# From experts to attention batch by batch: the order of norm, K, Q and V at the turn between two layers

## The chip, the cores and the metric

The kernel runs on one core of a Trainium2 chip. The metric is the device time in microseconds, the median of three executions. The engines are PE (matrix multiply), DVE (vector), ACT (scalar), POOL (GpSimd) and SP (here it issues DMAs only). Each takes its instructions in the order in which they are written, and they meet through semaphores.

## The reference

Two layers over x of shape (2, 512, 256). Layer 0 is a Mamba-2 block multiplied by a mixture of 8 experts; layer 1 is attention with rope, 32 query heads and 8 key and value heads of width 64, multiplied by a sign network.

```
xn = layernorm(x)
s = ssm(xn)                       # chunked selective scan
g = silu(experts(xn))             # top 2 of 8
x = x + s * g                     # end of layer 0
xn = layernorm(x)
q, k, v = xn @ Wq.T, xn @ Wk.T, xn @ Wv.T
q, k = rope(q), rope(k)
attn = softmax(causal(q @ k.T / sqrt(64)))
s = (attn @ v) @ Wo.T
a = sign(layernorm(x) * gamma + beta)
g = silu((a @ sign(W - mean(W)).T + bias) * alpha)
x = x + s * g
```

## The kernel before

Tokens lie in 8 tiles of 128 rows (`NT`), four to each of the two batches. Matmuls that need fp32 accuracy are split in three (`split3`): a value is written as a high and a low part, ACT copies the high part out of a PSUM bank, DVE or POOL subtracts it from the value for the low part, and PE multiplies low by high, high by low and high by high.

At the turn from layer 0 to layer 1 PE sums the experts' rows for four pairs of tiles (`sum_pair`), ACT applies silu to each pair (`gated`), DVE multiplies with the scan's result and adds to x (`add_pair`), and takes the statistics of the norm (`pair_stats`, `norm_spread`). The square root is ACT's, between DVE's `rsqrt_asked` and `rsqrt_made`. DVE then writes all 8 tiles of xn1; PE turns them (`turn_norm`), ACT and DVE make xnT_hi and xnT_lo (`lower_norm`). PE then makes K, Q and V of batch 0 for the first head group, then K and V of batch 1, and only then attention begins.

Attention is `attend(now, steps)`, called for each of the 8 head groups (a key head and its four query heads). All engines walk the same list `schedule(kind)`; each takes from it the operations that are its own. A step has a number and a priority, and the list is sorted by both. "Sab" is a matmul of scores for pair a (two heads of a batch; pairs 2 and 3 are batch 1), step b of 5. E is the exponential on ACT, N the reciprocal on DVE and the normalization on POOL, T the turn of prob on PE with its p_hi copy on ACT and p_lo on DVE, A the product with V. Beside these run the preparations: Q, r, a, h, l are the matmuls, rope, addition, high part and low part of later queries; Kh and Kl the high and low part of k_exp, which SP brings by DMA; Kq, Kr, Ka make K of head groups 4 to 7; KW and VQ split weights, F and G prepare the sign network's rows. `x_roped` says that a bank of PE has been taken by rope, and PE may not write it before.

SP's queue has a fixed order too: `spread_k` copies k to the four partition groups of k_exp (four DMAs), `store_k` and `store_v` put K and V in DRAM for later groups, `move_q` moves q_hi and q_lo to the layout qT (eight DMAs each), `load_wq` brings weights. In the first group of before batch 1's q is moved after all of these.

Of the kernel before, what the change touches and what calls it, by code (L numbers as in the profile page):

```python
# [72 lines left out]
def schedule(kind):  # L73

    own = [(14, 0, "VO", 0, 0), (1, 8, "Kh", 1, 0), (2, 6, "Kl", 1, 0)]
# [19 lines left out]
    if kind == "first":  # L95
        ready += [(0, 7, "KW", 0, 0), (3, 0, "VQ", 0, 0)] + half(1, 0, 1) + half(2, 7, 0) + half(3, 13, 0)
        for b in range(BATCH):
            n = 3 + 7 * b
            for k in range(2):
                ready += [(n + k, 8.2, "Kq", b, k), (n + k + 1, 8.2, "Kr", b, k), (n + k + 4, 6.2, "Ka", b, k)]  # L100
        ready += [(1 + t, 8.95, "F", t, 0) for t in range(NT)]
# [13 lines left out]
def side_by_side():  # L115
# [19 lines left out]
    z += [(4 * NJ + 0.5, "ACT", "kv", 0), (4 * NJ + 0.6, "POOL", "kv", 0)]  # L135
    z += [(4 * NJ + 0.1 * n, "DVE", "sum", n) for n in range(NT // 2)]
# [27 lines left out]
def layered_kernel(nc, x, params, consts, select, rope, w_in, w_out, w_moe, w_moe_tail, w_qkv, w_o, w_sign, out):  # L164
# [4 lines left out]
    with ctx:  # L169
# [301 lines left out]
        def _(sp):  # L471
# [74 lines left out]
            def move_q(g, b):  # L546

                hh = g * 2 + b
                for src, done in ((q_hi, qhi_done), (q_lo, qlo_done)):
# [14 lines left out]
            def spread_k(g, b):  # L564

                hh = g * 2 + b
                if hh > 0:
                    sp.wait_ge(klo_done, hh)
# [51 lines left out]
            move_q(0, 1)  # L620
# [30 lines left out]
        def _(dve):  # L651
# [22 lines left out]
            def rsqrt_asked(src, eps):  # L674
                TS(root_arg, src, eps, None, ALU.add).then_inc(var_ready, 1)

            def rsqrt_made(dst, ready=None):

                roots[0] += 1
                dve.wait_ge(root_ready, roots[0])  # L680
                then(vec.reciprocal(dst, root))
                then(TT(sv[:, 3, :], root_arg, dst, ALU.mult))
                then(TT(sv[:, 3, :], sv[:, 3, :], dst, ALU.mult))
                then(TS(sv[:, 3, :], sv[:, 3, :], -0.5, 1.5, ALU.mult, ALU.add))
                if ready:
                    TT(dst, dst, sv[:, 3, :], ALU.mult).then_inc(ready, 1)
                else:
                    then(TT(dst, dst, sv[:, 3, :], ALU.mult))
# [5 lines left out]
            root_arg, root = sv[:, 0, :], sv[:, 2, :]  # L694
# [326 lines left out]
            def attend(now, steps):  # L1021
                for late, op, i, k in steps:
# [22 lines left out]
                    elif op == "O":  # L1045
                        b, m = i // 2, i % 2
                        dve.wait_ge(ohi_done, q + 1)
                        TT(o_lo[:, b, m, :], bank[4 + m][:, :], o_hi[:, b, m, :].bitcast(F32), ALU.subtract).then_inc(olo_done, 1)  # L1048
# [17 lines left out]
            dve.wait_ge(turns_ready, 1)  # L1066
            dve.wait_ge(vpad_ready, 4)
            lower_norm(0)
            lower_norm(1)
            for k in range(2):  # L1070
# [5 lines left out]
            lower_norm(2)  # L1076
# [5 lines left out]
            ins.then_inc(q_first, 1)  # L1082
            lower_norm(3)
            TT(q_lo[:, :, :], q_mix[:, :, 0, :], q_hi[:, :, :].bitcast(F32), ALU.subtract).then_inc(qlo_done, 2)
            for k in range(2):
                rope_k(0, 1, k, bank[4 + k])
            rsqrt_made(rrms, second_ready)
            for b in range(BATCH):
                lower_v(0, b)
# [20 lines left out]
        def _(act):  # L1110
            actv = nc.scalar.activation

            def root(n):
                act.wait_ge(var_ready, n + 1)
                actv(sv[:, 2, :], sv[:, 0, :], ACT.Sqrt).then_inc(root_ready, 1)
# [125 lines left out]
            for n in range(NT // 2):  # L1241
                act.wait_ge(mixed, n + 1)
                actv(gate_y(n), gate_y(n), ACT.Silu).then_inc(gated, 1)
                if n == 1:
                    act.wait_ge(turns_full, 1)
                if n > 0:
                    ins = actv(turns[:, n - 1, :], bank[n - 1][:, :], ACT.Copy)
            ins.then_inc(turns_ready, 1)
            actv(sv[:, 8, :], ones[:, 0:NT], ACT.Sqrt)
            act.wait_ge(turns_full, 2)  # L1250
            actv(wsT[:, :, :], bank[4][:, :].rearrange("p (k o) -> p k o", k=KC), ACT.Copy).then_inc(turns_ready, 1)
# [17 lines left out]

            def upper_k(now, i):  # L1270
# [6 lines left out]
            def attend(now, steps):  # L1277
                for late, op, i, k in steps:
# [3 lines left out]
                    if op == "E":  # L1282
# [4 lines left out]
                        if k == 0 and isinstance(g, int) and q < 2:  # L1287
                            act.wait_ge(k_out[q], 16)
# [50 lines left out]
            root(2)  # L1339
            split_wq(0)  # L1340
            for k in range(KC * BATCH):
                b, c = k // KC, k % KC
# [629 lines left out]
```

## Time and profile before

| what | us |
|---|---|
| median of 3 runs | 773.09 |
| lowest, highest | 772.72, 774.26 |
| the profiled execution | 774.21 |
| its span | 772.4 |
| PE busy | 716.3 (93%) |
| DVE busy | 487.4 (63%) |
| ACT busy | 416.8 (54%) |
| POOL busy | 397.1 (51%) |

Mean granted clock 0.982. The span is the time from the first to the last instruction. Busy shares are means over stages; the expert stage takes about the first 300 us, and the attention groups fill the time from 345 us to the end.

### The profile page before, as it was taken

How to read it: one execution, taken by the hardware profiler on the slowest of the kernel's cores; microseconds unless marked ns; L12 is line 12 of the kernel's file. 1: busy time of each engine (PE TensorE's matmuls, PEld its weight loads, DVE VectorE, ACT ScalarE, POOL GpSimd, SP SyncE). 2: the span in 40 equal slices, each digit the busy share in tenths (PEclk: the TensorE clock that was granted, in tenths of full speed). 3: DMA queues.
4: the chain of work that ended last, by engine and by line, in shares of the span. 5: the costliest groups of instructions: out<-in, count | busy, mean ns of one | idle time of the engine just before them, and what ended most of it. 6: DMA issues, size and time to landing. Idle time of an engine off the chain costs nothing.

```text
span 772.4 us, 13448 instructions
## 1 busy us (share of the span) xinstructions
PE 716.3 (93%) x4575; PEld 625.0 (81%) x4576; DVE 487.4 (63%) x1030; ACT 416.8 (54%) x1043; POOL 397.1 (51%) x449
## 2 busy tenths in 40 slices
PE   2999999999999998588789999999999999999995
PEld 2887989989989986566678888888888888888883
DVE  7582655334332437876557777777777778777764
ACT  4446244134144133447367777667766677667663
POOL 1412442422332323118577786767867778677460
PEclk9899999999999999899899999999999999999999
DMA  8075977776877744154134222332223322232001
GB/s 295 31 249 183 277 251 233 246 245 203 280 241 214 244 98 118 27 168 121 60 94 112 58 63 65 84 89 52 64 63 90 85 55 64 52 90 56 1 1 55
DMA packets 103828, 98.06 MB, mean 127 GB/s; under 512 B 50576, under 2 KB 74064, under 8 KB 103632
## 3 DMA queue, kind: packets, MB, share of 16 engines
q1 hardware_dynamic: 101648, 91.43, 40.8%
q0 software_dynamic: 2112, 5.77, 2.3%
q8 instruction: 37, 0.61, 0.3%
q14 instruction: 31, 0.25, 0.1%
HBM read 69.24 MB, written 11.14 MB: 104 GB/s over the span
## 4 chain that ended last, share of the span: by engine, by line
PE 63%; DVE 12%; POOL 10%; ACT 8%; issue 4%; SPq 2%; DMA 1%; DVEq 0%; ACTq 0%; POOLq 0%
PE bank L1656 14%; PE bank L1516 8%; PE bank L1690 7%; PE bank L1517 7%; PE bank L1518 7%; PE bank L1512 7%; POOL prob L1474 5%; ACT prob L1290 3%; PE bank L1796 3%; DVE nmax L1035 2%; PE bank L1797 2%; POOL q_lo L1486 2%; ACT p_hi L1297 2%; DVE o_lo L1048 1%; POOL wq_lo L1454 1%
## 5 line engine op out<-in xcount | busy, mean ns | idle before, releaser
L1474 POOL TENSOR_TENSOR prob<-prob,rinv 128x128 f32<-128x128 f32 (+3 forms) x256 | 177.6, 724 | 102.9 <-DVE rinv L1040 102.9
L1290 ACT ACTIVATE prob<-bank,nmax 128x512 f32<-128x512 f32 (+3 forms) x256 | 133.2, 528 | 45.3 <-DVE nmax L1035 43.8
L1044 DVE TENSOR_TENSOR p_lo<-bank,p_hi 128x512 fp32r<-128x512 f32 x160 | 110.0, 687 | 52.8 <-ACT p_hi L1297 51.9
L1297 ACT ACTIVATE p_hi<-bank 128x512 fp32r<-128x512 f32 x160 | 96.3, 602 | 79.3 <-PE bank L1512 79.3
L1656 PEld LDWEIGHTS bank<-xgT,wm 128*128 128x128 f32 x920 | 108.7, 192 | 4.5 <-issue 2.9
L1656 PE MATMUL bank<-xgT,wm 128*128 128x128 f32 x920 | 111.3, 275 | 0.5 <-ACT xgT L1199 0.5
L1512 PE MATMUL bank<-cst,prob 128*128 128x128 f32 x640 | 97.9, 276 | 3.0 <-POOL prob L1474 1.2
L1035 DVE TENSOR_REDUCE nmax<-bank 128x1 f32<-128x512 f32 (+2 forms) x192 | 91.0, 502 | 12.7 <-PE bank L1799 12.1
L1516 PE MATMUL bank<-p_hi,v_lo 128*128 128x128 f32 (+3 forms) x256 | 93.0, 363 | 0.3 <-DVE p_lo L1044 0.3
L1796 PE MATMUL bank<-kT,qT 128*128 128x512 f32 (+3 forms) x256 | 82.2, 326 | 11.6 <-ACT prob L1290 6.0
L1445 POOL DMA_INDIRECT y_rows<-y_row,to_row x21 | 22.7, 1081 | 118.3 <-DVE y_row L904 92.6
L1518 PE MATMUL bank<-p_hi,v_hi 128*128 128x128 f32 (+3 forms) x256 | 82.4, 322 | 0.0
L1517 PE MATMUL bank<-p_lo,v_hi 128*128 128x128 f32 (+3 forms) x256 | 82.3, 322 | 0.0
L1512 PEld LDWEIGHTS bank<-cst,prob 128*128 128x128 f32 x640 | 73.7, 142 | 6.0 <-POOL prob L1474 3.3
L1797 PE MATMUL bank<-kT,qT 128*128 128x512 f32 (+3 forms) x256 | 74.7, 323 | 0.0
L1796 PEld LDWEIGHTS bank<-kT,qT 128*128 128x128 f32 x256 | 48.4, 189 | 21.8 <-issue 7.6
L1224 ACT ACTIVATE sil<-bank 128x512 f32<-128x512 f32 x23 | 13.7, 596 | 76.0 <-PE bank L1656 54.5
L1690 PE MATMUL bank<-wm,hE 128*128 128x256 f32 x230 | 53.5, 379 | 1.2 <-DVE y_low L909 1.2
L1290 ACT ACTIVATION_READ_ACCUMULATOR prob<-bank,nmax 128x1 f32 x256 | 52.4, 205 | 0.0
L944 DVE TENSOR_TENSOR hE<-sil,bank 128x512 f32<-128x512 f32 x23 | 15.8, 687 | 57.6 <-PE bank L1656 40.6
L1797 PEld LDWEIGHTS bank<-kT,qT 128*128 128x128 f32 x256 | 48.6, 190 | 3.9
L1518 PEld LDWEIGHTS bank<-p_hi,v_hi 128*128 128x128 f32 x256 | 48.4, 189 | 2.8
(307 smaller groups left out, 1544.6 us busy)
## 6 DMA issues: line engine op xcount, KB each, us to landing
wm<-in_w_moe SPq DMA_DIRECT2D x23, 1280.0 KB
wm<-in_w_moe SPq DMA_DIRECT2D x23, 640.0 KB
qT<-q_hi SPq DMA_DIRECT2D x124, 64.0 KB, 2.0
qT<-q_lo SPq DMA_DIRECT2D x124, 64.0 KB, 2.0
k_exp<-k_rows SPq DMA_DIRECT2D x56, 64.0 KB, 2.0
wtl<-in_w_moe_tail SPq DMA_DIRECT2D x46, 64.0 KB
y_rows<-gate SPq DMA_DIRECT2D x1, 2048.0 KB, 14.1
wq_raw<-in_w_qkv SPq DMA_DIRECT2D x32, 64.0 KB, 2.5
```

What stands on the lines that cost most here:

```text
L1044: TT(p_lo[:, b_, :], bank[2 + b_ % 2][:, :], p_hi[:, b_, :].bitcast(F32), ALU.subtract).then_inc(plo_done, 1)
L1290: ins = actv(prob[:, i % 2, h, POFF[j]:POFF[j] + (j + 1) * P], bk[:, at:at + (j + 1) * P], ACT.Exp, bias=nmax[:, i % 2, h, j:j + 1], accum ...
L1297: actv(p_hi[:, b_, :], bank[2 + b_ % 2][:, :], ACT.Copy).then_inc(phi_done, 1)
L1474: ins = GT(seg, seg, rinv[:, i % 2, k, j:j + 1].to_broadcast([P, (j + 1) * P]), ALU.mult)
L1512: return nc.tensor.transpose(dst, src, ident)
L1516: mm(dst, w_l, m_h, start=start, stop=False)
L1517: mm(dst, w_h, m_l, start=False, stop=False)
L1518: return mm(dst, w_h, m_h, start=False, stop=stop)
L1656: ins = mm(dst, w(c), xgT[:, u, c, :], start=c == 0, stop=c == KC - 1)
L1690: ins = mm(bank[3][:, 0:C], hE[:, u, i * P:(i + 1) * P], wm[:, s, i, PJ:WM] if i < FULL else ptl[:, s, :], start=i == 0, stop=i == HC - 1)
L1796: mm(dst, qs, kT[:, b, 0, 0:n], start=(h, j, at) == SCORES[k][0], stop=False)
L1797: mm(dst, qs, kT[:, b, 1, 0:n], start=False, stop=False)
```

## The change

The norm of layer 1 is split in halves, one for each batch. `half_norm` and `half_rows` do for four tiles what `norm_spread` and the loop over xn1 did for eight; batch 0's statistics, root and rows stand before the addition of pair 3, batch 1's after the rope of batch 0's K and Q. PE turns batch 0, makes its K, Q and V, turns batch 1 and begins attention. K and V of batch 1 are steps of the first group (K1, R1, A1, Vp, V1). The lows of wk0 go from POOL to DVE and those of wv0 behind xn's first half. Turns of the rope tables and their ACT copies stand behind the sums and gates of all pairs. The addition of batch 1's first q goes from POOL to DVE. SP moves q_hi of batch 1 before it spreads K of batch 1, and q_lo after. Kh and Kl of batch 1 go from steps 1 and 2 to 7 and 8, KW from 0 to 5, Kq from 3 and 10 to 8 and 14. K of batch 1 gets an area of its own (`k1_mix`, over o_lo).

```
-    own = [(14, 0, "VO", 0, 0), (1, 8, "Kh", 1, 0), (2, 6, "Kl", 1, 0)]
+    own = [(14, 0, "VO", 0, 0)]
+    own += [(7, 8, "Kh", 1, 0), (8, 6, "Kl", 1, 0)] if kind == "first" else [(1, 8, "Kh", 1, 0), (2, 6, "Kl", 1, 0)]
...
+        ready += [(1, 8.9, "R2", 0, 0), (1, 8.6, "V1", 0, 0), (6, 8.6, "V1", 1, 0)]
+        for k in range(2):
+            ready += [(1 + k, 8.1, "K1", 1, k), (2 + k, 8.1, "R1", 1, k), (3 + k, 6.1, "A1", 1, k)]
+        ready += [(2 + t - TB, 8.3, "Vp", t, 0) for t in range(TB, NT)]
...
-    z += [(4 * NJ + 0.1 * n, "DVE", "sum", n) for n in range(NT // 2)]
+    z += [(4 * NJ + 4 * (n // BATCH) + 0.1 * n, "DVE", "sum", n) for n in range(NT // 2)]
...
             store_v(0)
+            load_wq(1)
+            move_q(0, 1, (0,))
+            spread_k(0, 1)
             store_k(0, 1)
-            spread_k(0, 1)
+            move_q(0, 1, (1,))
             store_v(1)
-            load_wq(1)
...
-            move_q(0, 1)
...
+            def half_norm(b):
+                ts = slice(b * TB, (b + 1) * TB)
+                dve.wait_ge(stat_ready, NT + (b + 1) * TB)
+                for t in range(b * TB, (b + 1) * TB):
+                    vec.bn_aggr(mv[:, t, :], stats[:, t, :]).then_inc(aggr_ready, 1)
+                dve.wait_ge(aggr_ready, NT + (b + 1) * TB)
+                rsqrt_asked(mv[:, ts, 1], 1e-5, ts)
+
+            def half_rows(b):
+                rsqrt_made(rstd, None, slice(b * TB, (b + 1) * TB))
+                for t in range(b * TB, (b + 1) * TB):
+                    TS(xn1[:, t, :], x_tok[:, t, :], mv[:, t, 0:1], rstd[:, t:t + 1], ALU.subtract, ALU.mult).then_inc(xn_ready, 1)
...
+                        if q == 0:
+                            dve.wait_ge(k_out[1], 16)
+                            dve.wait_ge(k_in, 2 * K_MOVES)
...
+                    elif op == "a" and now == 0 and i == 1 and k == 0:
+                        dve.wait_ge(x_roped[1], 2)
+                        TT(q_mix[:, :, 0, :], q_mix[:, :, 0, :], q_mix[:, :, 1, :], ALU.add).then_inc(qadd_done, 2)
...
-            for k in range(KC * BATCH):
-                turn_norm(k, xn_ready, bank[k])
+            turn_half(0)
             pe.wait_ge(lo_done, KC * BATCH + 2)
             pe.wait_ge(w_lo_done, 4)
...
             for t in range(TB):
                 make_v(t)
-            pe.wait_ge(lo_done, 2 * KC * BATCH)
-            pe.wait_ge(kx_roped, 2)
-            for k in range(2):
-                make_k(0, 1, k, bank[4 + k])
-            for t in range(TB, NT):
-                make_v(t)
+            turn_half(1)
...
+                        if q < 2 and k == 0:
+                            pe.wait_ge(v_copied, NT)
```

The order of PE around the begin of attention. Before, the last V matmuls of batch 0 are followed by K of batch 1:

```order
L1516 MATMUL bank<-wv_hi,xnT_lo 128x512
L1517 MATMUL bank<-wv_lo,xnT_hi 128x512
L1518 MATMUL bank<-wv_hi,xnT_hi 128x512
L1516 MATMUL bank<-xnT_hi,wk_lo 128x512 [waits kx_roped,lo_done]
L1517 MATMUL bank<-xnT_lo,wk_hi 128x512
```

After, they are followed by the turns of batch 1 and the first scores (kT, qT):

```order
L1563 MATMUL bank<-wv_hi,xnT_lo 128x512
L1564 MATMUL bank<-wv_lo,xnT_hi 128x512
L1565 MATMUL bank<-wv_hi,xnT_hi 128x512
L1559 MATMUL bank<-cst,xn_132 128x128 [waits xn_ready]
L1559 MATMUL bank<-cst,xn_132 128x128
L1559 MATMUL bank<-cst,xn_132 128x128 [waits xn_ready]
L1559 MATMUL bank<-cst,xn_132 128x128
L1559 MATMUL bank<-cst,xn_132 128x128 [waits xn_ready]
L1559 MATMUL bank<-cst,xn_132 128x128
L1559 MATMUL bank<-cst,xn_132 128x128 [waits xn_ready]
L1559 MATMUL bank<-cst,xn_132 128x128
L1851 MATMUL bank<-kT,qT 128x512 [waits klo_done,q_first,exp_done,v_copied,mask_ready]
```

The 36 matmuls of K and V of batch 1 moved behind the first scores.

The order of ACT in the first group. Before, the high part of batch 1's K (kT<-k_exp) comes after the second exponential:

```order
L1290 ACTIVATE prob,rsum<-bank,nmax 128x384 [waits max_ready]
L1290 ACTIVATE prob,rsum<-bank,nmax 128x128
L1275 ACTIVATE kT<-k_exp 128x512 [waits k_in]
L1327 ACTIVATE xn_132<-xn_132,sv 128x256 [waits second_ready]
L1290 ACTIVATE prob,rsum<-bank,nmax 128x256 [waits max_ready]
```

After, it comes behind the exponential of the eighth score step, ahead of a p_hi copy:

```order
L1342 ACTIVATE p_hi<-bank 128x512 [waits av_done,pt_full]
L1335 ACTIVATE prob,rsum<-bank,nmax 128x256 [waits max_ready]
L1335 ACTIVATE prob,rsum<-bank,nmax 128x256
L1320 ACTIVATE kT<-k_exp 128x512 [waits k_in]
L1376 ACTIVATE xn_132<-xn_132,sv 128x256 [waits second_ready]
L1342 ACTIVATE p_hi<-bank 128x512 [waits av_done,pt_full]
L1335 ACTIVATE prob,rsum<-bank,nmax 128x512 [waits max_ready]
```

Its place moved six steps down.

The order of SP's queue. Before, k_exp of batch 1 (source prob) comes early and q_hi of batch 1 last:

```order
L601 DMA v_rows<-v_all 128x4x512 [waits v_copied]
L562 DMA k_rows<-prob 256x1x512 [waits kadd_done]
L571 DMA k_exp<-prob 32x512 [waits klo_done]
L571 DMA k_exp<-prob 32x512 x3
L601 DMA v_rows<-v_all 128x4x512 [waits v_copied]
L585 DMA wq_raw<-in_w_qkv 128x4x32 [waits wqlo_done]
L585 DMA wq_raw<-in_w_qkv 128x4x32 x3
```

After, it is behind the weights and the eight moves of q_hi:

```order
L611 DMA v_rows<-v_all 128x4x512 [waits v_copied]
L595 DMA wq_raw<-in_w_qkv 128x4x32 [waits wqlo_done]
L595 DMA wq_raw<-in_w_qkv 128x4x32 x3
L564 DMA qT<-q_hi 32x512 [waits qhi_done]
L564 DMA qT<-q_hi 32x512 x7
L581 DMA k_exp<-k_mix 32x512 [waits klo_done,kadd_done]
L581 DMA k_exp<-k_mix 32x512 x3
L570 DMA k_rows<-k_mix 256x1x512 [waits kadd_done]
L564 DMA qT<-q_lo 32x512 [waits qlo_done]
L564 DMA qT<-q_lo 32x512 x7
```

The two moves of q now enclose the transfer of batch 1's K.

## Rows read from the trace of the kernel before

**Rows 1.** Busy time by stretch, all engines; then clock, DMA share, GB/s.
```profile
390.00:402.00 12.00, 9.09 (x64) 7.53 (x63) 6.73 (x13) 6.04 (x20) 11.70 (x13) 1.00 0.26 68
550.00:600.00 50.00, 49.37 (x317) 43.07 (x316) 37.88 (x75) 35.40 (x99) 38.17 (x45) 1.00 0.28 70
```

**Rows 2.** Waits of PE from 296 to 346 us: total, times, longest.
```profile
PE bank L1512 <- DVE xn L988: 7.9, 1, 7.9
PE bank L1516 <- DVE xnT_lo L997: 2.4, 1, 2.4
PE bank L1722 <- DVE y_low L909: 1.1, 1, 1.1
```

**Rows 3.** Waits of PE from 340 to 402 us.
```profile
PE bank L1796 <- DMA qT<-q_lo: 4.7, 1, 4.7
PE bank L1512 <- DVE q_mix L1002: 2.9, 2, 1.8
```

**Rows 4.** PE by stretches of 2 us: busy, clock, DMA share, GB/s.
```profile
314.00:316.00 2.00, 0.00 (x0) 0.51 0.00 0
...
374.00:376.00 2.00, 2.00 (x9) 0.50 0.11 42
...
378.00:380.00 2.00, 2.00 (x13) 0.77 0.00 0
```

**Rows 5.** Instructions in order of time, 305 to 346 us: start, duration, idle before.
```profile
305.08 0.60 ACT L1247 ACTIVATE turns<-bank 128x512 f32<-128x512 f32 x1 [0.73 <-PE bank L1512]
...
315.47 2.67 DVE L988 TENSOR_SCALAR xn<-x_tok,mv,sv 128x256 f32<-128x256 f32 x8
...
320.35 0.74 PE L1516 MATMUL bank<-xnT_hi,wk_lo 128*128 128x512 f32 x1
...
321.39 1.28 ACT L1346 ACT_TABLE_LOAD   x1
...
327.62 2.51 SPq L571 DMA_DIRECT2D k_exp<-prob  x4
327.80 1.23 DVE L1075 TENSOR_TENSOR q_mix<-q_mix 128x1024 f32<-128x1024 f32 x1
...
330.65 2.54 ACT L1353 ACTIVATE qT<-q_mix 32x512 fp32r<-32x512 f32 x4
...
333.92 1.27 POOL L1458 TENSOR_TENSOR kT<-k_exp,kT 128x512 fp32r<-128x512 f32 x1 [6.32 <-ACT kT L1275]
334.20 2.07 DVE L1084 TENSOR_TENSOR q_lo<-q_mix,q_hi 128x1024 fp32r<-128x1024 f32 x1
...
345.38 0.47 PE L1796 MATMUL bank<-kT,qT 128*128 128x512 f32 x1 [0.83 <-ACTq L1363]
```

**Rows 6.** The same, first head group, 345 to 398 us.
```profile
345.95 0.47 PE L1516 MATMUL bank<-xnT_hi,wq_lo 128*128 128x512 f32 x1
...
347.42 0.34 PE L1796 MATMUL bank<-kT,qT 128*128 128x384 f32 x1
...
349.07 0.58 ACT L1290 ACTIVATE prob<-bank,nmax 128x384 f32<-128x384 f32 x1
...
353.75 0.68 DVE L1001 TENSOR_TENSOR v_all<-bank,turns 128x512 f32<-128x512 f32 x1
...
355.01 2.75 POOL L1474 TENSOR_TENSOR prob<-prob,rinv 128x128 f32<-128x128 f32 x4
...
357.82 0.66 PE L1512 MATMUL bank<-cst,prob 128*128 128x128 f32 x4 [1.20 <-POOL prob L1474]
...
360.25 1.06 ACT L1268 ACTIVATE q_hi<-q_mix 128x1024 fp32r<-128x1024 f32 x1 [3.45 <-POOL q_mix L1483]
...
361.34 4.95 SPq L556 DMA_DIRECT2D qT<-q_hi  x8
...
397.71 0.66 PE L1512 MATMUL bank<-cst,xn 128*128 128x128 f32 x4 [1.80 <-DVE q_mix L1002]
```

**Rows 7.** The chain that ended last, at 371 us: start, duration, what.
```profile
371.02 2.04 DMA qT<-q_lo
```

More of the change, by code:

```diff
@@ L374, in layered_kernel @@
         o_hi = attn("o_hi", [P, 2, 2, HALF], F32R)
+        k1_mix = Map(attn.at)("k1_mix", [P, 2, 2, HALF])
         o_lo = attn("o_lo", [P, 2, 2, HALF], F32R)
         def k_mix(r, b):
+            if r == 0 and b:
+                return k1_mix[:, :, :, :]
             if r == 0:
@@ L544, in _, with move_q @@
             sp.wait_ge(s_part, NT)
-            def move_q(g, b):
+            def move_q(g, b, parts=(0, 1)):
                 hh = g * 2 + b
-                for src, done in ((q_hi, qhi_done), (q_lo, qlo_done)):
+                for src, done in [((q_hi, qhi_done), (q_lo, qlo_done))[i] for i in parts]:
                     at = 0 if src is q_hi else 2
@@ L672, in _, with rsqrt_asked, rsqrt_made @@
             roots = [0]
-            def rsqrt_asked(src, eps):
-                TS(root_arg, src, eps, None, ALU.add).then_inc(var_ready, 1)
-            def rsqrt_made(dst, ready=None):
+            def rsqrt_asked(src, eps, ts=slice(0, NT)):
+                TS(sv[:, 0, ts], src, eps, None, ALU.add).then_inc(var_ready, 1)
+            def rsqrt_made(dst, ready=None, ts=slice(0, NT)):
+                arg, more, to = sv[:, 0, ts], sv[:, 3, ts], dst[:, ts]
                 roots[0] += 1
                 dve.wait_ge(root_ready, roots[0])
[L681 to L684, printed above, removed]
+                then(vec.reciprocal(to, sv[:, 2, ts]))
+                then(STT(out=more, in0=to, scalar=-0.5, in1=arg, op0=ALU.mult, op1=ALU.mult))
+                then(TT(more, more, to, ALU.mult))
+                last = STT(out=to, in0=more, scalar=1.5, in1=to, op0=ALU.add, op1=ALU.mult)
                 if ready:
-                    TT(dst, dst, sv[:, 3, :], ALU.mult).then_inc(ready, 1)
+                    last.then_inc(ready, 1)
                 else:
-                    then(TT(dst, dst, sv[:, 3, :], ALU.mult))
+                    then(last)
             def rsqrt(dst, src, eps):
@@ L1082, in _ @@
             ins.then_inc(q_first, 1)
+            lower_norm(2)
             lower_norm(3)
             TT(q_lo[:, :, :], q_mix[:, :, 0, :], q_hi[:, :, :].bitcast(F32), ALU.subtract).then_inc(qlo_done, 2)
-            for k in range(2):
[L1086 to L1089, printed above, removed]
             attend(0, schedule("first"))
@@ L1243, in _, with turned @@
                 actv(gate_y(n), gate_y(n), ACT.Silu).then_inc(gated, 1)
[L1244 to L1248, printed above, removed]
-            actv(sv[:, 8, :], ones[:, 0:NT], ACT.Sqrt)
-            act.wait_ge(turns_full, 2)
-            actv(wsT[:, :, :], bank[4][:, :].rearrange("p (k o) -> p k o", k=KC), ACT.Copy).then_inc(turns_ready, 1)
+            actv(sv[:, 8, :], ones[:, 0:NT], ACT.Sqrt)
+            def turned():
+                act.wait_ge(turns_full, 2)
+                actv(wsT[:, :, :], bank[4][:, :].rearrange("p (k o) -> p k o", k=KC), ACT.Copy)
+                for i in range(3):
+                    ins = actv(turns[:, i, :], bank[i][:, :], ACT.Copy)
+                ins.then_inc(turns_ready, 1)
             def split_wq(g):
@@ L1349, in _ @@
             upper_q(0, 0)
+            root(3, slice(TB, NT))
+            upper_k(0, 0)
             for i in range(2):
@@ L1354, in _ @@
             ins.then_inc(q_first, 1)
-            upper_k(0, 0)
-            for t in range(2, NT):
-                copy_v(t)
-            act.wait_ge(vpad_ready, 4)
-            for b in range(BATCH):
-                ts = slice(b * TB, (b + 1) * TB)
-                act.wait_ge(v_copied, (b + 1) * TB)
-                actv(v_hi[:, ts, HD:2 * HD], v_all[:, ts, 0:HD], ACT.Copy).then_inc(vhi_done, 1)
+            copy_v(2)
+            copy_v(3)
+            upper_norm(1)
+            root(4)
+            actv(sv[:, 8, :], ones[:, 0:NT], ACT.Exp)
             act.sem_inc(exp_done, 2)
@@ L1498, in _ @@
             lower_k(0, 0)
-            for k in range(2):
-                add_k(0, 1, k)
             attend(0, schedule("first"))
```

134 lines of the change are left out of this document (85 added, 49 removed).

## The prediction

> **What bounds the kernel now.** I read the busy time by stretch first. From 550 to 600 us the matmul engine is busy 49.4 of 50 us at full clock; from 390 to 402 it is busy only 9.1 of 12 while POOL works 11.7 [rows 1]. So the attention groups after the first are bound by the matmul engine, and a delay or a gain at the end of the first group goes straight to the end. All that the change touches lies between 298 and 402 us, and there the engine has gaps. The waits of the matmul engine name them: 7.9 us for the normalized rows xn, 2.4 us for xnT_lo of the second batch, 1.1 us for y_low [rows 2]; in the first group 4.7 us for the transfer of q_lo, 2.9 us for q_mix [rows 3], 1.2 us for prob [rows 6]. That is 20 us. A second loss goes with them: the clock granted in the gap is 0.51 at 314 us, 0.50 at 374 us after the 4.7 us wait, and back at full between 378 and 380 us [rows 4]; 0.5 is the 1.2 GHz level of the two, 1.0 the 2.4 GHz level.
>
> **How I count.** The chain is followed in order of each engine's instructions, each with its duration in the trace, to four points that both kernels share. I write "Sab" for the scores of pair a, step b. Before: first K matmul at 320.35, S00 at 345.38 [rows 5], S20 (first scores of batch 1) at 371.02 + 2.04 = 373.1 [rows 3, 7], end of G10, the second turn of the sign rows, 398.1 (its turns begin at 397.71 [rows 6]).
>
> **Part 1, up to K.** DVE writes y_low before the sums of pairs 2 and 3, so PE's 1.1 us wait goes [rows 2]: PE is through with the sums at about 308.0 instead of 309.1. wk_lo on DVE has no row; between half of q_mix's 1.23 us, 0.6, and the whole of q_lo's 2.07 [rows 5] I take 0.7, by the nearer. It puts off the first add by 0.6 us. Norm of batch 0 alone: two adds per pair, four statistics, then rows at 0.33 us each (2.67 us for 8) instead of eight rows [rows 5]. They are ready at about 311.1 (with the dearer wk_lo 312.1). But ACT now does gates 2 and 3, the 1.28 us table load, the first wq copy, wsT and the three turns copies at 0.60 us [rows 5] before PE may turn anything: 306.5 + 0.6 + 1.3 + 0.4 + 0.6 + 0.6 + 1.8 = 311.8. ACT's copies, not the norm, end this wait. Eight turns (1.8 at the lower clock), two hi copies, two lo subtractions: K starts at 315.9, **4.45 us earlier**.
>
> **Part 2, up to S00.** K, Q, V of batch 0 take 11.6 us as before, so PE is at 327.5 and turns batch 1 by 329.6. It then waits for ACT. Counted from kadd: the four k_exp issues 2.51 and landing 2.04 [rows 5, 7] give k_in at 327.7; ACT then does kT 0.6, the qT copies 2.54, two V copies 1.1, two hi copies 1.2, the root 0.2 and the Exp table load 1.28 + 0.2: 335.0 to 335.2 [rows 5]. Only then is exp_done raised. So S00 at **335.0, 10.4 us earlier**, with PE idle 5.4 us before it, and K1 and V of batch 1 (36 matmuls at 0.235, 8.5 us) still to be done. The 2.4 us wait of rows 2 goes, and this one stands in its place: net 1.9 us at this point.
>
> **Part 3, S00 to T00 (first turn of prob).** Before it was 12.4 us. Now, from S00 as zero: a score step takes PE 0.57, six matmuls 1.47 (345.38, 345.95, 347.42) [rows 5, 6]. PE's own work up to S11 is done at 15.4. But DVE has from S01 on six scores' maxima, four rope pairs at 1.28 [rows 6], q_mix at 1.23 [rows 5], lower_v 0.4 and the small ops 0.9: S04's maximum at 13.7. ACT follows: exponentials of S04 to 14.75 (a two part one 1.0), V copy, xn2, E10 to 16.7, the wk copies 1.3, q_hi 1.06 [rows 6] to 19.1, and the last V copy to 19.7. T00 now waits for all eight V copies. T00 at 19.75, that is **354.8, 3.0 us earlier** than 357.8 [rows 6], while 12 matmuls of Kq (2.8 us) that stood before it are now behind: even. PE is idle 4.3 us.
>
> **Part 4, T00 to S20.** SP issues q_hi of batch 1 first: 8 at 0.62 are 4.95 us [rows 6], then spread_k(0,1) 2.5, landing 2.04: k_in at 19.1 + 9.6 = 28.7. On ACT the Kh of batch 1 stands behind the third exponentials of pair 1, reached at 24.5. It is an in-order engine, so it waits 4.3 us, and behind it are the p_hi copy of T02 and E13. Before, that Kh found its data at once. What waits for ACT: p_lo on DVE at 31.2, then N10 and rope of Q20 to 32.6, and PE's Kq00, which now stands right behind Q21 (done at 26.2): PE idle 6.4 us. Then Kq00, S14, T03, A01 to 35.9, and Kq01 waits for the rope of Q21, behind S14's maximum and T03's p_lo: 37.85. S20 at 39.3, that is 335.0 + 39.3 = **374.3, 1.2 us later** than 373.1. The q_lo transfer, now landed at 34.4, no longer sets it.
>
> **Part 5, S20 to G10.** Before 25.0 us, 2.6 of them lost to the lower clock [rows 4]. Now PE needs 12 us up to Q31, but POOL needs N11 2.75, two adds 2.5, kT 1.27, Ka 1.27, N20 2.75, two q_lo 2.5 [a normalization is 2.75, rows 6] from 2.5 us on, plus a rope: 17.4. Kq10 stands right behind Q31 and waits for that rope: 5 us. Before, the sign turns were what waited there, 1.1 and 1.8 us in all, with eight other steps already done. Kq11 waits 2.0 us more, and G10 1.4 for the rope of Kq11. From S20 27.9 us: **2.9 us more**.
>
> **Sum.** 1.2 + 2.9 = 4.1 us later, before the clock. Gaps of 5.4 and 6.4 us are as long as those after which rows 4 show half clock for 4 to 5 us after work resumes (320.35 is still low, 378 too); matmuls that the chain waits for are then some 1.5 + 2.5 us late, if all of it counts, nothing if DVE and ACT hide it; I take 1. The profiled execution took 774.21 us (span 772.4), so it would take 779.3; the median of the runs is 773.09, so I forecast **778.5 us**. The cost of the DVE wait for k_out1 at the first o_lo, and of the new k1_mix area, is nothing: both transfers land 10 us before. Bounds of the unknown: PE waits and the lower clock fully hidden, 1.2 - 2.6 + 774 = 772; everything in full, 4.1 + 4 + 2 = 783.
>
> **A port.** q_lo on DVE took 2.07 us beside a POOL subtraction of 1.27 us that had started 0.28 us earlier, where q_mix of the same size alone took 1.23 [rows 5]. The Trainium skill, page "SBUF — State Buffer", section "Who interferes with whom", says that a DVE instruction with two SBUF inputs and a GpSimd one that reads SBUF exclude each other for the whole instruction. The trace agrees: the end of q_lo is the end of POOL plus 1.1. The change moves the q_mix addition of batch 1 from POOL to DVE, beside POOL's wq_lo and normalization. By the row alone I price it at 1.23. By the rule it could cost up to 1.3 us more on the chain of part 3, and the sum would be 779.8; I leave it out since POOL by my count is still waiting for wq then.
>
> **Rivals.**
> 1. The gaps are filled (faster). K1 and V of batch 1 are 8.5 us of work laid into a group that had 8.8 us of named gaps, and S00 is 10.4 us earlier. For it: [rows 1, 3]. It needs ACT to reach Kh after k_in, that is the in-order wait of part 4 to be absent; then S20 is bound by q_lo at 335 + 34.4 = 369.4, 3.7 us earlier, and with part 5 even the time is 769.4. With every gap filled it gains 10.4 - 8.5 + 8.8 = 10.7 us: 762.4; half of that, 767.7, is as far as I let the range go. Against it: the queue order on SP, eight issues of 0.62 us ahead of spread_k. 0.29.
> 2. Nothing (within 0.2%, 1.5 us, about what a measurement can tell from none): the 3.7 us of rival 1 and the 2.9 us of part 5 cancel: 772 to 774.5. 0.09.
> 3. The forecast, 774.6 to 781: 0.47.
> 4. The clock. PE is left idle five times for about 4 us and more (3.8, 5.4, 4.3, 6.4, 5) instead of twice, and each stretch after it runs at 0.5; then the matmuls of parts 3 and 4 are on the chain and it is 781 to 785. For it, rows 4; against it, PE has slack there. 0.15.
>
> So faster 0.29, same 0.09, slower 0.62. Range 767 to 783.
>
> **What would show it.** Right: K from about 316, S00 near 335 with an idle of some 5 us before it ended by ACT; T00 near 355 released by an ACT V copy; an idle of ACT of 3 to 5 us before a kT copy, ended by the k_exp transfer; PE waiting 4 to 7 us for DVE's q_mix before wk matmuls, twice; S20 at 373 to 378. Wrong: if the kT copy finds its data there, if S20 is at 370 or before, or if the matmuls of the wk half follow Q without a wait. If S00 is later than 338, part 2 is what failed.

## The result, and the profile after

The changed kernel takes 783.74 us against 772.90 us (medians of four executions of each), ratio 1.0151 (95% interval 1.0126 to 1.0177): 10.8 us slower. I had forecast 778.5 us, range 767 to 783. The sign was right, the size was half of it, and the median lies just outside the range. The profiled execution took 783.04 us, its span is 781.2 us against 772.4, mean granted clock 0.977 against 0.982.

The waits of PE in the changed kernel, in the order of the three stretches 296 to 330, 330 to 372 and 372 to 420 us (total, times, longest), to be laid beside [rows 2, 3]:

```profile
PE bank L1559 <- ACT turns L1288: 3.0, 1, 3.0
PE bank L1563 <- DVE xnT_lo L1008: 1.8, 1, 1.8
PE bank L1559 <- DVE xn L1002: 1.4, 2, 0.8
...
PE bank L1563 <- DVE q_mix L1013: 5.4, 2, 4.1
PE bank L1851 <- DVE qT L1123: 3.0, 1, 3.0
PE bank L1559 <- ACT v_all L1299: 2.9, 1, 2.9
...
PE bank L1563 <- DVE q_mix L1013: 7.4, 2, 6.0
PE bank L1559 <- DVE v_all L1013: 1.3, 1, 1.3
```

The 7.9 us for xn [rows 2] and the 4.7 us for q_lo [rows 3] are gone. In their place stand three waits of some 3 us (turns, qT, v_all) and four before the wk matmuls (L1563 <- q_mix, 12.8 us). PE's clock in stretches of 2 us (busy, clock, DMA share, GB/s), to be laid beside [rows 4]:

```profile
328.00:330.00 2.00, 0.00 (x0) 0.73 0.00 0
330.00:332.00 2.00, 1.09 (x3) 0.50 0.00 0
332.00:334.00 2.00, 2.00 (x6) 0.50 0.00 0
...
364.00:366.00 2.00, 2.00 (x5) 0.50 0.40 98
366.00:368.00 2.00, 2.00 (x8) 0.50 1.02 397
368.00:370.00 2.00, 2.00 (x10) 0.53 0.33 127
...
392.00:394.00 2.00, 2.00 (x6) 0.50 0.90 328
394.00:396.00 2.00, 2.00 (x9) 0.50 0.39 98
```

After the waits for qT (3.0 us) and before the wk matmuls (4.1 and 6.0 us) PE works 5 to 6 us at 1.2 GHz (granted clock 0.50 of full), with full busy time and fewer matmuls: 5 to 10 in 2 us.

One table holds the study. It takes the starts of three score steps in each profiled execution: S00, S20 (batch 1's first scores) and S00 of the next head group ("next"). The last column is what remains to the end of the span. "First y_lo" is the start of DVE's first y_lo in the expert stage, far ahead of the norm, K, Q and V that the change reorders; it shows how late an execution already was there.

| kernel | ratio to before, interval | first y_lo | S00 | S00 to S20 | S20 to next | next to end |
|---|---|---|---|---|---|---|
| before | | 91.74 | 345.38 | 27.7 | 33.1 | 366.2 |
| changed | 1.0151 (1.0126 to 1.0177) | 89.90 | 330.91 | 42.0 | 38.4 | 369.9 |
| changed, again | 1.0165 (1.0135 to 1.0195) | 89.81 | 331.96 | 41.9 | 39.7 | 369.7 |
| wk steps back | 0.9962 (0.9950 to 0.9974) | 89.73 | 330.72 | 36.6 | 33.1 | 366.4 |
| only batch 0's back | 1.0103 (1.0078 to 1.0127) | 91.35 | 333.80 | 35.9 | 39.5 | 369.8 |
| only batch 1's back | 1.0035 (1.0015 to 1.0054) | 89.77 | 330.79 | 42.1 | 32.1 | 366.0 |
| store last | 1.0140 (1.0113 to 1.0167) | 89.75 | 332.19 | 41.9 | 39.7 | 369.3 |
| additions behind | 1.0238 (1.0219 to 1.0258) | 89.86 | 331.46 | 41.7 | 40.5 | 376.2 |
| additions and store behind | 1.0132 (1.0101 to 1.0164) | 89.88 | 332.29 | 41.7 | 40.5 | 366.4 |
| v_lo later | 1.0152 (1.0130 to 1.0173) | 89.80 | 332.17 | 42.0 | 39.8 | 369.8 |
| K and V before the scores | 1.0020 (1.0007 to 1.0032) | 89.79 | 345.30 | 28.5 | 33.1 | 366.3 |
| lows moved, in before | 1.0003 (0.9988 to 1.0018) | 90.22 | 343.75 | 27.8 | 33.0 | 366.4 |
| wk back, spread first | 0.9968 (0.9952 to 0.9984) | 89.68 | 332.14 | 36.4 | 32.7 | 366.4 |
| the same, filled | 0.9976 (0.9960 to 0.9992) | 89.63 | 332.04 | 36.4 | 32.7 | 366.3 |
| wk back, early q | 0.9901 (0.9878 to 0.9924) | 93.19 | 334.25 | 32.2 | 31.6 | 366.4 |
| the same, and kT | 0.9866 (0.9845 to 0.9887) | 89.83 | 332.04 | 30.7 | 31.4 | 366.4 |

The changed kernel is 14.5 us ahead at S00, loses 14.3 us up to S20, 5.3 us up to the next group, and 3.7 us after it. But 1.8 of the 14.5 us are not the change's. The first y_lo of the kernel before, of the kernel before with the lows moved, of the changed kernel, and of the run with early q:

```profile
91.74 0.68 DVE L890 TENSOR_TENSOR y_lo<-gate,y_hi 128x512 fp32r<-128x512 f32 x1
```

```profile
90.22 0.68 DVE L890 TENSOR_TENSOR y_lo<-gate,y_hi 128x512 fp32r<-128x512 f32 x1
```

```profile
89.90 0.68 DVE L901 TENSOR_TENSOR y_lo<-gate,y_hi 128x512 fp32r<-128x512 f32 x1
```

```profile
93.19 0.68 DVE L901 TENSOR_TENSOR y_lo<-gate,y_hi 128x512 fp32r<-128x512 f32 x1
```

Kernels with the same code up to this row differ here by up to 3.6 us, so this is a difference between executions. Taken off, the changed kernel is 12.6 us ahead at S00, and 14.3 + 5.3 + 3.7 - 12.6 makes 10.6 us slower, which agrees with the 10.8 us of the medians. S00 is comparable between rows of the table only with the first y_lo subtracted.

### The profile page after: what moved, and what is told of

It reads as the page before. It is cut to its first block, busy times and chain, and to the rows that moved or that the text cites. A ratio compares the mean times of both kernels' runs of the same rounds, so it can differ in the third digit from the quotient of the medians.

```text
span 781.2 us, 13456 instructions
## 1 busy us (share of the span) xinstructions
PE 719.2 (92%) x4575; PEld 626.9 (80%) x4576; DVE 486.0 (62%) x1033; ACT 416.9 (53%) x1044; POOL 393.6 (50%) x446
## 4 chain that ended last, share of the span: by engine, by line
PE 64%; DVE 12%; POOL 9%; ACT 8%; issue 4%; DMA 1%; SPq 1%; DVEq 0%; ACTq 0%
PE bank L1703 14%; PE bank L1737 8%; PE bank L1563 8%; PE bank L1564 7%; PE bank L1565 7%; PE bank L1559 7%; POOL prob L1519 5%; ACT prob L1335 3%; PE bank L1851 3%; DVE nmax L1046 3%; PE bank L1852 2%; POOL q_lo L1531 2%; ACT p_hi L1342 2%; DVE o_lo L1062 2%; DVE q_mix L1012 1%
## 5 line engine op out<-in xcount | busy, mean ns | idle before, releaser
L1563 PE MATMUL bank<-p_hi,v_lo 128*128 128x128 f32 (+3 forms) x256 | 93.2, 364 | 0.3 <-DVE p_lo L1055 0.3
```

Source lines behind the costliest of these rows:

```text
L1563: mm(dst, w_l, m_h, start=start, stop=False)
```

## The experiments

**The wk steps.** The step table again as before for the second K projection:

```
-        ready += [(5, 7, "KW", 0, 0), ...
-            n = 8 + 6 * b
+        ready += [(0, 7, "KW", 0, 0), ...
+            n = 3 + 7 * b
```

> The changed kernel with the steps of the second K projection (matmuls, rope, additions) and of the wk split where they stood in the kernel before (3 + 7b and 0 instead of 8 + 6b and 5). Theory (places of the projection): the two waits of PE before those matmuls of batch 1 (6.0 and 1.4 us) go and the K additions are done before group 1, so 2.9 us of the stretch from S20 to G10 and the 2.6 us in group 1 come back: 778 us. Rival (resources): the same ropes, additions and 24 matmuls only press into the first steps, where K and V of batch 1 now stand; PE waits there for wk_low and for rope, and it is not faster: 784 to 788 us.

Measured 770.12 us, ratio 0.9962: 13.6 us under the changed kernel's 783.74, 8 us better than the theory said, and faster than the kernel before. These step numbers, of the second K projection and of the wk split, are what made the change slow. Its waits from 296 to 420 us:

```profile
PE bank L1851 <- POOL kT L1503: 5.8, 1, 5.8
...
PE bank L1559 <- DVE q_mix L1013: 2.9, 2, 1.8
```

No wait before the wk matmuls (L1563 <- q_mix) is in the list any more. Then each batch alone, `n = 3 + 11 * b` (wk split at 0) and `n = 8 + 2 * b`:

> The changed kernel with the second K projection of batch 0 (matmuls, rope, additions) back at step 3 and the wk split at step 0, as before, but that of batch 1 left at step 14. With both back, S20 came at 367.34 instead of 372.95 and S00 of group 1 at 400.43 instead of 411.34. Theory (two terms of like size): the batch 0 part is worth the 5.6 us up to S20, the batch 1 part the rest, 5.3 us up to group 1 and 2.6 us in it; this kernel then has S20 near 367.5, waits 5 to 6 us before the wk matmuls of batch 1 and takes 783.7 - 5.6 = 778.1 us. Rival (only the late additions count): S20's gain is eaten by the next POOL chain, and it takes 782 us or more.

> The changed kernel with only the second K projection of batch 1 back at step 10; batch 0 stays at step 8 and the wk split at 5. Theory (two terms): S20 stays at 373 or is up to 2 us later, since matmuls and ropes of both batches now stand close together behind Q of pair 2, but the wait of 6.0 us before the wk matmuls of batch 1 after Q31 goes, and POOL's additions end before group 1, so its T03 turn does not wait for prob: 783.7 - 5.3 - 2.6 + 1 = 777 us. Rival (crowding): the two projections together push S20 as far as the later wait was long; 783 us.

Measured 781.08 us and 776.41 us. In the table batch 0's return is worth 6.1 us between S00 and S20; batch 1's 6.3 us between S20 and the next group, and 3.8 us after it. Two separate terms, as the theory said, the second the larger. The first median lies between the theory (778.1) and its rival (782 or more): by the ratios (1.0103 against 1.0151) batch 0's return is worth 3.7 us, not 6.1. Of the 6.1 us 1.1 are given back in the next stretch (39.5 against 38.4), and from the first y_lo to S00 this execution took 242.5 us where the changed kernel's took 241.0 and, when repeated, 242.2: scatter, whose cause stays open. The second median is near its theory (777), but its 12 runs lie in two bunches 4 us apart, and its row in the table is of the faster.

**The loss behind the first group.** In the changed kernel the last steps of the wk work end up in group 1. POOL and ACT there (start, duration, idle before); v_all<-v_all are the two additions of K, which has its area there:

```profile
411.14 2.76 POOL L1519 TENSOR_TENSOR prob<-prob,rinv 128x128 f32<-128x128 f32 x4 [8.47 <-DVE rinv L1051]
413.86 1.30 POOL L1508 TENSOR_TENSOR v_all<-v_all 128x512 f32<-128x512 f32 x1
415.10 2.55 POOL L1531 TENSOR_TENSOR q_lo<-q_mix,q_hi 128x512 fp32r<-128x512 f32 x2
417.61 1.28 POOL L1508 TENSOR_TENSOR v_all<-v_all 128x512 f32<-128x512 f32 x1
418.85 1.29 POOL L1499 TENSOR_TENSOR wq_lo<-wq_raw,wq_hi 128x512 fp32r<-128x512 f32 x1
420.10 2.75 POOL L1519 TENSOR_TENSOR prob<-prob,rinv 128x128 f32<-128x128 f32 x4
...
423.48 0.63 ACT L1320 ACTIVATE kT<-k_exp 128x512 fp32r<-128x512 f32 x1 [5.82 <-DMA k_exp<-k_rows]
```

Two rows on SP's queue stand between the second addition (v_all) and that kT copy:

```profile
418.92 0.58 SPq L570 DMA_DIRECT2D k_rows<-v_all  x1
419.54 2.27 SPq L581 DMA_DIRECT2D k_exp<-k_rows  x4
```

So two suspects: the queue (the spread stands behind a store that waits for an addition) and POOL's order (the additions stand ahead of a normalization, that of the second head of pair 3, for which PE waits 2.6 us). First the queue:

```
-            store_k(1, 1)
             spread_k(1, 1)
             load_v(1, 1)
             load_wo(1)
+            store_k(1, 1)
```

> The changed kernel with one thing altered: on the SP queue the store of the last K quarter (second four head groups, batch 1) stands behind the K spread, the V load and the wo load of group 1, not ahead of them. Theory (queue): in group 1 ACT waited 5.8 us for k_exp only because that store waits for POOL's last K addition and the spread stands behind it; then k_exp lands some 3 us earlier, the POOL normalization and the turns of group 1 no longer slip, and the time falls by the 2.6 us which the milestones of group 1 lost between S03 and S04 (+5.1 to +7.7): 781.1 us, ratio to the changed kernel 0.9966. Rival (POOL): the four K additions now stand in POOL's order so late that its first normalization of group 1 is late whatever the queue does; then 783.7 us.

Measured 784.19 us, the rival's time: no gain. ACT's wait of 5.8 us is gone from its trace, the prob wait still has 2.6 us. My theory of the queue fell; next to end it is worth 0.4 to 0.6 us. Then POOL's additions of batch 1 moved behind a normalization in group 1, the store still last:

```
                         ins.then_inc(prob_ready, 1)
+                        if now == 1 and not late and q == PAIRS and k == 0:
+                            for j in range(2):
+                                add_k(1, 1, j)
```

> The changed kernel with its late second K projection kept, the last K store behind the loads of group 1 on SP (as in the run with the store last), and besides the two K additions of batch 1 on POOL behind the first normalization of group 1 instead of ahead of it. The run with the store last took ACT's 5.8 us wait for k_exp away and gained nothing. Theory (POOL's order): the 2.6 us wait of PE for prob in group 1 comes from q_lo, two additions and wq_lo ahead of that normalization; without the additions it ends 2.5 us earlier, the wait is 0 to 0.3 us and the time 783.7 - 2.6 = 781.1 us (the rest of what is lost lies before group 1). Rival: the wait only moves to the next normalization, or to kT low behind it, and the time stays at 783.7 us.

Measured 791.68 us. The prob wait went, but neither theory came: this condition puts the additions one normalization later than I meant (at 428.66), the store waits for them, and the eight moves of q_hi that stand behind it on SP start at 434.29. PE then:

```profile
445.81 0.79 PE L1854 MATMUL bank<-kT,qT 128*128 128x512 f32 x1 [7.81 <-DMA qT<-q_lo]
```

It shows the queue's price when something is needed behind it. Last, the additions directly behind the normalization that PE waits for, and the store behind the whole of group 1's queue:

> The changed kernel with its late second K projection kept, its two K additions of batch 1 on POOL directly behind the normalization that PE waits for in group 1 (second head of pair 3), and the K store that needs them behind the whole DMA order of group 1 on SP. Theory (POOL's order is the cause of that wait, SP's queue only passes a late addition on): the prob wait of 2.6 us goes, no wait for q_lo comes (8 issues start near 423 as in the changed kernel), and the time is 2.6 us under the changed kernel on the same chip, 781 us. Rival (the wait moves to the following normalization or kT low, which the additions now delay by 2.5 us): no gain, 783.7 us.

> The changed kernel itself, on the chip of the run beside it. Expected: 783.7 us, ratio to the kernel before 1.0151. If it is 782 or below or 786 or above, the differences of 1 to 3 us that I took between runs of different chips need their intervals read with more care.

Measured 782.07 and 785.23 us. Waits of PE from 404 to 470 us, first of the changed kernel again, then of this one:

```profile
PE bank L1559 <- POOL prob L1519: 2.6, 1, 2.6
PE bank L1851 <- ACT prob L1335: 1.7, 4, 0.7
PE bank L1559 <- DVE v_all L1013: 1.3, 1, 1.3
```

```profile
PE bank L1563 <- DVE v_all L1014: 1.3, 1, 1.3
PE bank L1855 <- ACT prob L1336: 1.0, 3, 0.5
```

The repeated changed kernel lies within the 782 to 786 us that I had set. Next to end is 366.4 us, as before, where it is 369.3 with the store alone moved and 369.7 in the changed kernel again. So the loss behind the first group is POOL's order, but for the 0.4 us of the store. The medians fall by 3.2 us, near the theory's 2.6, but their intervals (1.0135 to 1.0195 and 1.0101 to 1.0164) overlap: it is the distance in the traces that shows it. S20 to next is 0.8 us longer in this run; that was not followed up.

**The wait at kT.** v_lo of batch 1 on DVE at step 11 instead of 6:

> The changed kernel with one DVE instruction moved: v_lo of batch 1 at step 11 instead of step 6. Beside POOL's q_lo it took 3.30 us instead of about 0.4. Theory (my prediction's part 4): the maximum of S12 comes 2.9 us earlier, but ACT then reaches its kT copy earlier and waits there for k_exp, 3 to 4 us instead of 0.83; the time stays within 0.5 us of the changed kernel: 783.7 us. Rival (the port is the chain): the queue was not the limit, S20 comes 2.5 to 3 us earlier and the time is 781 us.

Measured 785.19 us, the changed kernel's time within the intervals. The two kernels' rows for v_lo and kT, changed kernel first:

```profile
354.53 3.30 DVE L1024 TENSOR_TENSOR v_lo<-v_all,v_hi 128x256 fp32r<-128x256 f32 x1 [0.60 <-ACT v_hi L1313]
...
360.32 0.63 ACT L1320 ACTIVATE kT<-k_exp 128x512 fp32r<-128x512 f32 x1 [0.83 <-DMA k_exp<-k_mix]
```

```profile
362.24 0.63 ACT L1320 ACTIVATE kT<-k_exp 128x512 fp32r<-128x512 f32 x1 [4.09 <-DMA k_exp<-k_mix]
...
379.10 0.77 DVE L1024 TENSOR_TENSOR v_lo<-v_all,v_hi 128x256 fp32r<-128x256 f32 x1
```

The wait of 4.3 us that I predicted is there (4.09) as soon as v_lo is out of the way. It needs no edit, though: in the second profiled execution of the changed kernel, with v_lo in its old place, v_lo took 0.83 us and the wait is there too:

```profile
356.14 0.83 DVE L1024 TENSOR_TENSOR v_lo<-v_all,v_hi 128x256 fp32r<-128x256 f32 x1 [0.59 <-ACT v_hi L1313]
```

```profile
361.93 0.63 ACT L1320 ACTIVATE kT<-k_exp 128x512 fp32r<-128x512 f32 x1 [3.29 <-DMA k_exp<-k_mix]
```

In all three the k_exp transfer releases the copy, 29.4 to 30.1 us after S00. A slow v_lo only makes ACT come to it later.

**The first half of the change alone.** Norm by batch, but K and V of batch 1 before the scores, step table and SP order as before:

> The changed kernel up to the turns of batch 1 (y_low and the wk and wv lows moved, sums first, norm by batch), but K and V of batch 1, their ropes and copies stand before the first scores again, and the step table of the first group and SP's queue order are those of the kernel before. It tells what the first half of the change is worth alone. Theory: K starts at 312.3, K1 and V of batch 1 take 8.5 to 9 us after the turns, S00 comes at 340 instead of 345.4, the first group runs as in the kernel before: 773 - 5.4 = 767.5 us. Rival (chain of ACT): the second table load, the copies of V and the first POOL lows stand one behind the other on ACT before the first exponential, S00 at 344 or later: 771.5 to 773 us.

Measured 774.58 us, ratio 1.0020 (1.0007 to 1.0032), slower than theory and rival had it. S00 comes at 345.30; counted from the first y_lo that is 1.9 us later than before. PE's waits from 296 to 420 us:

```profile
PE bank L1566 <- DVE xnT_lo L1003: 6.0, 2, 4.2
PE bank L1854 <- DMA qT<-q_lo: 4.7, 1, 4.7
```

K began at 312.19, and this early start is spent on a wait for batch 1's lows; DVE does batch 1's norm only after batch 0's ropes. And the lows moved off the expert stage, in the kernel before (the lines `kv` and `sum` of the change and `lower_wk`):

> The kernel before with only the wk and wv lows of the first projection moved off POOL's place beside the last experts (wk low to DVE ahead of the adds, wv low on POOL behind the first norm row), and the sums of the expert rows of batch 1 four places later, as in the changed kernel. Theory: y_lo took 2.85 us beside POOL's wv low and took PE's 1.1 us wait with it; in the changed kernel it took 0.68 and the milestones there come about 2 us earlier. It carries to the end one for one or less by DVE's extra 0.7 us: 773 - 1.5 = 771.5 us. Rival: the norm of eight rows waits for DVE anyway, the wk low on DVE stands ahead of the adds, and nothing is gained: 773 us.

Measured 773.16 us: the same, as the rival said. The last y_lo took 0.68 us in its trace too, where it took 2.85 before. S00 came 1.6 us earlier, but the first y_lo already 1.5 us: the faster y_lo brought 0.1 us.

**From here on, better.** With the wk steps back, PE waits 5.8 us at S20. First the SP order:

```
-            move_q(0, 1, (0,))
             spread_k(0, 1)
             store_k(0, 1)
-            move_q(0, 1, (1,))
             store_v(1)
+            move_q(0, 1, (0, 1))
```

and kT low at (7, 9) instead of (8, 6); then, besides, batch 1's wk matmuls at step 9 and v_lo at 8:

> The kernel with the second K projection back (3 + 7b), and on SP's queue the K spread, K store and V store of batch 1 ahead of its q_hi and q_lo transfers, and the kT low of batch 1 on POOL ahead of the first normalization of pair 1. In the kernel it starts from, PE waits 5.8 us at S20 (367.34) for that kT low, which waits for k_exp (landed near 360.8) and stands behind a normalization. Theory (queue order): k_exp lands at 355.5 and kT low is done by 361; S20 is then bound by the q_lo transfer, issued 3 us after the present 360.1 at the latest, so S20 at 366.5 to 368: no more than 1 us either way, 769 to 771 us. Rival (kT was the only bound): S20 moves to 363 or before and the time to 766.

> The same as the run with the spread first, and besides the wk matmuls of batch 1 at step 9 instead of 10 (one of the two stands before S20 and fills the wait there) and v_lo of batch 1 at step 8 instead of 6, out of the way of POOL's q_lo. Theory (work laid into the wait): 1.4 us of matmuls go before S20 while PE waits there anyway, and S12's maximum comes 2 us earlier: 1 to 2 us faster than the run with the spread first, 768 to 769.5 us. Rival: the matmul stands in PE's order behind the rope of pair 2's Q and holds S20 up, as it did in the changed kernel: 771 us or more.

Measured 770.49 and 770.79 us, both the same as with the wk steps back alone: now q_lo ends the wait (6.3 and 5.9 us). The theory of the queue held in the first; in the second my 1 to 2 us did not come: PE still waits at S20, and the wait ends with the transfer. What sets the transfer is when q_hi is ready, and that copy stood at step 5 though its input was there 6 us earlier:

```
-             (n + 4, 6, "a", i, 1), (n + 5, 8, "h", i, 0)]
-        return z + [(n + 6, 6, "l", i, 0), (n + 6 + slow, 6, "l", i, 1)]
+             (n + 4, 6, "a", i, 1), (n + h, 8, "h", i, 0)]
+        return z + [(n + l, 6.2, "l", i, 0), (n + l + slow, 6.2, "l", i, 1)]
...  half(1, 0, 0) -> half(1, 0, 0, 3, 4)
```

> The kernel with the second K projection back (3 + 7b), and ACT's q_hi copy of batch 1 at step 3 instead of 5, POOL's q_lo of batch 1 at step 4 instead of 6. Its addition on DVE ends at 344.6 but the copy stood at 350.9, and the 16 issues of q_hi and q_lo at 0.62 us each, with spread_k between, then reach to 365.4 and set S20 together with kT low (367.24). Theory (queue): q_hi is issued from 345.6, spread from 351, k_exp lands at 355.5 instead of 360.8, q_lo lands at 361.5; kT low still stands behind the first normalization of pair 1 on POOL (rinv at 363 before, some 2 us earlier now): S20 at 364 to 365.5, 2 to 3 us earlier, 767.5 us. Rival: PE's slower clock after the wait, or the next POOL chain, takes it back: 769.5 to 770.5 us.

> The same as the run with q early, and kT low of batch 1 on POOL ahead of the first normalization of pair 1, and v_lo of batch 1 on DVE at step 9, out of the way of POOL's q_lo and normalization. Theory (nothing but PE's own work sets S20): PE arrives there at 361.5, q_lo lands at 361.5, kT low is ready by 360: S20 at 362 instead of 367.3, 5 us earlier, of which the normalizations of pairs 1 and 2 on POOL (2.75 us each) may take one or two: 765.5 us. Rival (POOL's normalization chain): S20 is early, but the turns of pair 1 wait for prob and S30 stays where it was: 768.5 us or more.

Measured 765.89 us (theory 767.5) and, with kT low at (7, 9) and v_lo at 9 as well, **762.49 us**, ratio 0.9866 (0.9845 to 0.9887): 10.5 us faster than the kernel before, the best of the study, and 3 us better than the theory's 765.5. In the first of the two S20 still waits 1.65 us, until POOL's kT low is done. From 360 to 370 us (PE, PEld, DVE, ACT, POOL busy, clock, DMA share, GB/s), first with the wk steps back alone, then this one:

```profile
360.00:370.00 10.00, 4.23 (x23) 3.51 (x22) 5.10 (x10) 4.92 (x13) 5.21 (x6) 0.81 0.65 218
```

```profile
360.00:370.00 10.00, 10.00 (x62) 8.73 (x62) 8.35 (x18) 5.72 (x18) 8.34 (x11) 1.00 0.51 167
```

S20 starts at 362.78 with no wait, and in this stretch the clock stays at 2.4 GHz.

## Why the prediction was right in sign and wrong in size

**Part 1, K 4.45 us earlier.** K came at 312.29, 8.1 us earlier, of which 1.8 us are the later start of the profiled execution before; 6.2 us remain. ACT's copies of turns ended the wait, as predicted (3.0 us). PE was through with sums and turns at 305.5; my 308.0 less the 1.8 us is 306.2. ACT's chain and the turns after it took 1.1 us less than I had. The last y_lo, with POOL's wv_lo (2.34 us) beside it before and alone after, is 2.2 us shorter, and I had not looked there; the run with the lows moved says that this is worth 0.1 us. Its row before and after:

```profile
293.87 2.85 DVE L890 TENSOR_TENSOR y_lo<-gate,y_hi 128x512 fp32r<-128x512 f32 x1
```

```profile
292.06 0.68 DVE L901 TENSOR_TENSOR y_lo<-gate,y_hi 128x512 fp32r<-128x512 f32 x1
```

**Part 2, S00 at 335.0.** It came at 330.9 (332.7 with the 1.8 us added, 2.2 us better than counted); from K on 18.6 us, where I had 19.1. DVE's qT lows ended the wait, not ACT's table load: 3.0 us instead of 5.4.

**Part 3, S00 to T00 19.75 us.** 21.0 us. V's last copy ended the wait, as predicted (2.9 us instead of 4.3). The 1.3 us more fit the clock: S00 to S01, the same matmuls, took 3.95 us at 0.50 where they took 2.04 before.

**Part 4, S20 39.3 us after S00.** 42.0. The in-order wait at kT was 0.83 us in one execution of the changed kernel, where v_lo took 3.30 us beside POOL's subtractions (q_lo x2, 2.51 us, among them), and 3.29 us in the other, where v_lo took 0.83; S20 came 42.0 and 41.9 us after S00. So the chain that I named, the k_exp transfer behind the eight moves of q_hi, was right, and v_lo changed only what filled the time before it. The wait before the wk matmuls was 4.1 us in the first and 5.7 us in the second (I had 6.4), but the six matmuls then took 2.73 us at 1.2 GHz instead of 1.4, and the scores and turns behind them as well.

The port rule of the Trainium skill that I had weighed and left out ("SBUF — State Buffer", "Who interferes with whom": a DVE instruction with two SBUF inputs and a GpSimd one that reads SBUF exclude each other) bore on another instruction than the one I named. The trace agrees with the rule. The q_mix addition took 1.19 us, and POOL's wq_lo, which began 0.4 us after it, 1.94 instead of 1.29. v_lo took 3.30 us instead of the 0.43 us of batch 0's v_lo, with POOL idle:

```profile
338.34 0.43 DVE L1024 TENSOR_TENSOR v_lo<-v_all,v_hi 128x256 fp32r<-128x256 f32 x1 [0.27 <-ACT v_hi L1313]
```

In the run with v_lo later it took 0.77 us, begun 0.5 us before a normalization of POOL ended. Which of the two engines is held differed between executions of one program: 3.30 and 0.83 us for the same v_lo, 2.51 and 2.73 us for POOL's two q_lo.

**Part 5, 27.9 us from S20 to G10's end.** The waits were those named: 6.0 us before the wk matmuls of batch 1 (5 predicted), 1.4 (2.0) and 1.3 (1.4). The row that shows it, DVE's rope held by POOL's q_lo:

```profile
389.81 0.69 DVE L1012 TENSOR_TENSOR q_mix<-bank,turns 128x512 f32<-128x512 f32 x1 [3.51 <-POOL q_lo L1531]
...
391.15 0.79 PE L1563 MATMUL bank<-xnT_hi,wk_lo 128*128 128x512 f32 x1 [6.04 <-DVE q_mix L1013]
```

G10 started at 403.94 and ended at 404.35, 31.4 us after S20, 3.5 us more than I had. The first wk matmul of batch 1 began 18.2 us after S20; my terms for it add up to 16.8, not to the 17.4 that I wrote, and POOL also stood idle 1.17 us for rinv.

**The sum.** In the profiles the changed kernel was 5.1 us late at the next group's S00, exactly my 4.1 + 1. That was luck twice over. First, 1.8 us of start hide in it; without them it was 7.0 us late. Second, a start 2.2 us better than counted met 2.7 and 3.5 us of more loss in parts 4 and 5, and behind G10 1.1 us came back. I took 1 us for the clock. By the rows it is 5 to 6, an estimate: from the first wk matmul to S20 9.1 us where I had 6.7, from the first wk matmul of batch 1 to the end of G10 13.2 where I had 10.5, both with the clock at 0.50 to begin with, and of the 1.9 us at S00 some are hidden later. Rival 4 was the better account of this term, and its range of 781 to 785 us holds the measured time; no run changed the clock alone. (773.09 + 5.1 is 778.2, not 778.5; that changes nothing.)

**The step that failed** is the first paragraph's "All that the change touches lies between 298 and 402 us", and with it "a delay or a gain at the end of the first group goes straight to the end", with nothing counted for K's two additions that the change moved from the first group's list into the time of the next. They stand on POOL, which is in order, ahead of a normalization that PE waits for. With the store that hangs on them that is 3.5 us (369.9 against 366.4), shown by the run with additions and store behind. Behind the first group the changed kernel lost 3.7 of the 5.5 us that I was short (10.6 against 5.1). The other 1.9 us are what the second mis-sized term, the clock, left after the better start.

Rival 1 described the kernel that the change could have been. The run with wk back and the spread first has its two conditions, no wait of ACT at kT and S20 bound by q_lo: S20 at 368.55 and 770.5 us, where I had 369.4 and 769.4. That the last run reaches 762.5 us, where I had 762.4 for every gap filled, is a coincidence: PE still waits 3.6 us for q_mix in its first group.

## What to carry to other kernels

Work laid into gaps has a place in each engine's order, and the price is paid where its consumers and the banks it holds stand: list for every moved matmul what must free its bank, and on which in-order engine that hangs. When a table of steps is shifted, look also at what drops over the end of its stage. A gap that a transfer ends was closed here at the transfer's first input, not by another order of the queue. And before times in two traces are compared, look at a point ahead of the change: here the traces differed there by 1.8 us already.

## What the runs showed of the hardware

Executions differ before the first y_lo by up to 3.6 us (89.63 to 93.19 in kernels with the same code up to there). They differ also by the clock in one gap. In the changed kernel PE waited 1.39 us up to 398.59 and worked on at full clock; in its other profiled execution the wait at that place was 1.98 us, the stretch after it is at 0.50, and S20 to the next group takes 39.7 us instead of 38.4. The two executions:

```profile
398.00:400.00 2.00, 1.41 (x6) 1.00 0.43 108
400.00:402.00 2.00, 2.00 (x18) 1.00 0.45 112
```

```profile
398.00:400.00 2.00, 0.77 (x3) 0.89 0.39 98
400.00:402.00 2.00, 2.00 (x6) 0.50 0.39 98
```

The 12 runs of the kernel with only batch 1's steps back lie in two bunches, 772.6 to 773.2 us and 776.4 to 777.3, and its profile is of the lower. What chooses between them stays open. The five runs of the best kernel lie within 2.1 us.
